# Slots without a loop, and mask products between two transpositions, in a fused "macaron" block

## What is computed

```python
def attn_layer(x, Wqkv, qs, ksc, Wo):            # x = shift_tokens(x)
    q, k, v = split(x @ Wqkv)                    # 16 heads of 64
    q, k = l2norm(q) * qs, l2norm(k) * ksc
    q, k = rotary with scale (q), rotary with 1/scale (k)
    # windows of 32: each query window sees its own and the previous key window
    sim = einsum('bhwie,bhwje->bhwij', q_win, k_two_wins) * 8.0
    sim = where(mask, -finfo.max, sim)           # i < j or i > j + 32
    out = softmax(sim) @ v_two_wins
    return out @ Wo
def ffn_layer(x, g, bln, W1, b1, W2, b2):
    a, gate = split((layernorm(x) * g + bln) @ W1 + b1)
    return a * gelu(gate) @ W2 + b2
for i in range(6):
    x = attn_layer(shift_tokens(x), ...) + x
    x = ffn_layer(shift_tokens(x), ...) + x
```

## Time and profile before

| | us |
|---|---|
| median of 3 runs | 3688.96 (3684.85 to 3690.24) |
| the profiled execution | 3686.52 |
| its span, first to last instruction | 3684.7 |
| PE busy | 3433.7 (93%) |
| DVE busy | 2845.5 (77%) |
| ACT busy | 2381.3 (65%) |
| POOL busy | 2333.4 (63%) |

### The profile page before, as it was taken

One profiled execution on the slowest core, in us unless ns is written; L12 is line 12 of the kernel. 1 busy time (PEld: TensorE's weight loads), 2 busy tenths in 40 slices (PEclk: granted clock), 3 DMA queues, 4 the chain that ended last, 5 costly groups with the idle time before them and its releaser, 6 DMA issues.

```text
span 3684.7 us, 129395 instructions
## 1 busy us (share of the span) xinstructions
PE 3433.7 (93%) x51660; PEld 1855.8 (50%) x51660; DVE 2845.5 (77%) x6042; ACT 2381.3 (65%) x4153; POOL 2333.4 (63%) x2187
## 2 busy tenths in 40 slices
PE   3799999999999999999797999999999999999997
PEld 2355554554554554555363555545545545545553
DVE  1788887887887887888367888878878878878883
ACT  1576776775776776677524667767767766766774
POOL 0677766766766776767145767667667766767661
PEclk6899999999999999999998999999999999999999
DMA  5000000000000000000100000000000000000000
GB/s 187 10 9 28 21 12 27 22 12 27 21 13 27 21 12 25 24 12 5 54 1 8 11 26 23 12 27 21 13 27 21 12 27 22 12 24 26 12 5 13
DMA packets 50151, 83.62 MB, mean 23 GB/s; under 512 B 7168, under 2 KB 37120, under 8 KB 47232
## 3 DMA queue, kind: packets, MB, share of 16 engines
q1 hardware_dynamic: 49536, 75.05, 6.5%
HBM read 67.69 MB, written 7.34 MB: 20 GB/s over the span
## 4 chain that ended last, share of the span: by engine, by line
PE 86%; issue 4%; DVE 4%; ACT 3%; POOL 1%; DMA 1%; SPq 0%; DVEq 0%; ACTq 0%; POOLq 0%
PE VS L890 19%; PE QA L830 18%; PE TB L849 10%; PE TB L914 7%; PE VS L937 7%; PE TB L873 6%; PE FB L963 3%; PE FB L964 3%; PE FB L972 3%; PE VS L928 2%; ACT KT L460 2%; PE TB L857 1%; PE FB L948 1%; PE FB L953 1%; DMA KT<-in_w_out 1%
## 5 line engine op out<-in xcount | busy, mean ns | idle before, releaser
L334 POOL TENSOR_TENSOR QN<-T 128x512 f32<-128x512 f32 x768 | 980.0, 1276 | 673.6 <-DVE T L606 673.6
L341 POOL TENSOR_TENSOR QN<-QN,RR 128x512 f32<-128x512 f32 x768 | 801.6, 1044 | 316.8 <-DVE RR L627 316.8
L830 PE MATMUL QA<-WQ,Y 128*128 128x512 f32 x1536 | 806.3, 622 | 68.7 <-DVE T L606 25.4
L890 PE MATMUL VS<-MW,Y 128*32 128x512 f32 x6144 | 738.8, 598 | 2.7 <-DVE Z L679 2.7
L446 ACT ACTIVATE SQ<-QA 128x512 f32<-128x512 f32 x768 | 458.6, 597 | 289.3 <-PE QA L830 254.5
L606 DVE TENSOR_TENSOR T<-QA,TAB 128x256 f32<-128x256 f32 x1536 | 571.0, 412 | 4.1 <-issue 4.1
L601 DVE TENSOR_TENSOR T<-QA,TAB 128x512 f32<-128x512 f32 x768 | 522.9, 681 | 48.2 <-issue 21.3
L466 ACT ACTIVATE V<-VS 128x512 f32<-128x512 f32 x768 | 461.1, 600 | 90.1 <-PE VS L890 89.5
L633 DVE TENSOR_TENSOR Y<-TB,Y 64x128 f32<-64x128 f32 x384 | 111.0, 289 | 521.0 <-PE TB L857 518.3
L614 DVE TENSOR_REDUCE SSQ<-SQ 128x8 f32<-128x512 f32 x768 | 486.8, 675 | 0.0
L914 PEld LDWEIGHTS TB<-CST,QN 128*128 128x128 f32 x3072 | 360.9, 142 | 220.9 <-issue 183.5
(11 more groups left out here) (172 smaller groups left out, 4260.2 us busy)
## 6 DMA issues: line engine op xcount, KB each, us to landing
TAB<-in_tables SPq DMA_DIRECT2D x192, 128.0 KB, 2.1
WQ<-in_w_qk SPq DMA_DIRECT2D x48, 256.0 KB, 3.2
MW<-m_dram SPq DMA_DIRECT2D x12, 1024.0 KB, 4.8
m_dram<-QN SPq DMA_DIRECT2D x6, 1024.0 KB, 4.9
W1R<-in_w SPq DMA_DIRECT2D x12, 341.0 KB, 3.4
KT<-in_w_vt SPq DMA_DIRECT2D x6, 512.0 KB, 5.8
KT<-in_w_out SPq DMA_DIRECT2D x6, 512.0 KB, 6.6
W<-in_w SPq DMA_DIRECT2D x12, 192.0 KB, 2.4
```

Of the source, the lines that this page charges most:

```text
L334: po.tensor_tensor(QN[:, n % 2, k, :], T1[:, k, :], T2[:, k, :], ALU.add).then_inc(s_add, 1)
L341: po.tensor_tensor(heads(QN[:, m % 2, k, :]), heads(QN[:, m % 2, k, :]), RR[:, m % 2, 8 * k:8 * k + 8].unsqueeze(2).to_broadcast([P, 8, DH ...
L830: mm(QA[:, k % 2, :], Y[:, j * P:(j + 1) * P], WQ[:, k, :], start=True, stop=True).then_inc(s_qk, 1)
L890: last = mm(VS[32 * q:32 * q + 32, w % 2, :], Y[:, a:a + WIN], MW[:, q, :], start=True, stop=True, tile_position=(0, 32 * q), skip_group_c ...
```

## The change

`all_slots` no longer has a loop: all 104 slots of a stack are written out, with constants in the waits. SyncE's conditions for the next layer's weights, which stood on the loop variable, are worked out from `c`, and `edge` is true for the same slots as before. Second, the two mask products leave `scores()` for a function of their own, `mask_scores()`, that is called right behind the transposition of the last keys and ahead of that of the last queries and of FFN-up. With them go the waits for VS (`s_ve`, and `s_z` in edge slots); the waits for the keys (`s_te3`, `s_kp`) stay in `scores()`.

```diff
         def all_slots(engine, slot, s):
-            for c in range(AHEAD):
-                slot(c, None, s)
-            with engine.Fori(0, DEPTH - 1) as it:
-                for c in range(AHEAD, AHEAD + TPL):
-                    slot(c, it, s)
-            for c in range(AHEAD + TILES - TPL, LAST):
+            for c in range(LAST):
                 slot(c, None, s)
...
-                if it is None:
+                if not AHEAD <= c < AHEAD + TILES - TPL:
                     return
-                nxt = bass.ds(it + 1, 1)
-                if c == AHEAD:
-                    sp.wait_ge(s_w1, by_layer(1, s * DEPTH, it, 1))
-                    sp.wait_ge(s_prb, by_layer(1, s * DEPTH, it, 1))
+                l = (c - AHEAD) // TPL + 1
+                nxt = slice(l, l + 1)
+                if c % TPL == AHEAD:
+                    sp.wait_ge(s_w1, by_layer(1, s * DEPTH + l - 1, it, 1))
+                    sp.wait_ge(s_prb, by_layer(1, s * DEPTH + l - 1, it, 1))
                     up_weights(nxt)
...
-                edge = it is None
+                edge = c < AHEAD or c >= AHEAD + TILES - TPL
...
+                def mask_scores():
+                    m = n - 2
+                    if edge:
+                        after(pe, s_z, 1, n - 3, 0, it, s)
+                    after(pe, s_ve, 4, n - 4, 3, it, s)
+                    for e in range(2):
+                        mm(VS[:, e, :].rearrange("p (a c k) -> p a c k", a=2, c=CH), IDB[:, :],
+                           MASKN[:, 0 if m % TPL == 0 else 1, :, :].unsqueeze(2).to_broadcast([P, 2, CH, WIN]),
+                           start=True, stop=False, skip_group_check=True)
+
                 def scores():
                     m = n - 2
                     j = m % 4
                     if j == 0 and m % TILES:
                         pe.wait_ge(s_kp, by_tile(1, m // 4, None) if it is None else it * 4 + m // 4)
-                    if edge:
-                        after(pe, s_z, 1, n - 3, 0, it, s)
-                    after(pe, s_ve, 4, n - 4, 3, it, s)
                     pe.wait_ge(s_te3, by_tile(1, m, it, 1))
-                    for e in range(2):
-                        mm(VS[:, e, :].rearrange("p (a c k) -> p a c k", a=2, c=CH), IDB[:, :],
-                           MASKN[:, 0 if m % TPL == 0 else 1, :, :].unsqueeze(2).to_broadcast([P, 2, CH, WIN]),
-                           start=True, stop=False, skip_group_check=True)
...
                 if live(c, 2, it):
                     qk_transpose(2, 3)
+                    mask_scores()
                 if live(c, 1, it):
                     qk_transpose(1, 2)
```

## The result

The changed kernel takes **3582.62 us** (median of four runs, 3580.02 to 3587.59), the kernel before 3689.6 us (median of its four runs beside it). The ratio is 0.9713 with a 95% interval of 0.9696 to 0.973. The forecast was 3581.0 us in a range of 3568 to 3615. The profiled execution took 3582.17 us, its span is 3580.4 us (3684.7 before).

What follows compares the result with a forecast made beforehand. PE, busy 93% of the span, was taken to bound the kernel. Terms: 70.1 + 42.8 - 3.8 - 6 + 4 = 107 us off the profiled 3686.52, giving 3579.5, as a median 3581 us; range 3568 to 3615.

Steps and rivals of the forecast that it cites:

- The branches: Slots behind the eight taken loop branches of PE: written out they become ordinary slots, 70.1 us gained.
- Rival 3: Branch slots: branches are cheap, the slot behind is long for a reason that stays; 3651 us, chance 0.03.
- The mask products: Masks moved between the two transpositions: 102 waits for the keys' copy go, 0.42 us each, 42.8 us gained.
- The thin margin of 0.11 us: Before the score products: PE arrives 1.40 us after the first transposition, keys' copy ends at 1.24, seen 0.05 later.
- rival 2: Mask's wait only changes place, keys' or V copy comes later; 42.8 us stay, costs paid; 3624 us, chance 0.07.
- The third cost: First FFN-up slot of each layer: attention products wait longer for the queries' copy, 12 x 0.5 = -6 us.
- Part three: Instruction fetch in written-out code: no new stalls before score products, half of the old ones gone, +4 us.
- rival 1: New written-out slots stall at the end slots' rate, 17 in 160 at 1.7 us, 28 us; 3613 us, chance 0.15.

Runs made afterwards that it cites:

- pe_looped: Kernel before with TensorE keeping its loop, the four other engines written out, mask products at their old place: 3654.64 us, ratio 0.9905.
- pe_written: Kernel before with only TensorE's slots written out, the other engines keeping their loop, mask products at their old place: 3678.86 us, ratio 0.9971.
- unroll_only: Changed kernel with the mask products back at their old place behind the wait for the last keys, slots written out: 3643.53 us, ratio 0.9876.
- split_waits: unroll_only with the two waits before the masks taken apart, only the second mask product waiting for the last keys: 3580.71 us, ratio 0.9693.

## Why the prediction was right, and where it was not

**The branches** were sized well: 70.1 us predicted, 72.0 measured over the eight slots, and its split between PE's standstill with a cold clock and DVE's own late code is what pe_looped (48.7 us) and pe_written (22.9 us) show. Rival 3, the cheap branch, is out: without the branches the slots are ordinary ones. The trace (3984 ns for a taken branch of PE, 76 ns for one that falls through) agrees with the Trainium skill's "Runtime: NRT & Kernel Launch" (Instruction fetch mechanics) that a branch out of the fetched window stalls.

**The mask products** gained what their term said: 0.42 or 0.43 us in each slot with centring or FFN-down, at a loss of 0.06 (predicted 0.04) in the others. The thin margin of 0.11 us before the score products held in all of them, so rival 2 is out. What the term missed is that their old place would have cost more in straight code than in the loop: unroll_only has 16 us more of extras, and 0.07 us more in 80 slots, that go away with the move. And split_waits shows that it need not have been a move: one wait per matmul at the old place does as well.

**The third cost** (12 x 0.5 = -6 us) failed as a step. "There I take 0.43 plus some 0.09" presumed that ScalarE's chain begins at the end of the FFN-up product with the table load, as the earlier trace rows show it for a loop slot. In straight code the load stands ahead of the wait. The trace of before had it: slot 9 to slot 10, already written out, takes 15.97 us where the loop's layers take 16.79. The order of ACT's instructions in the changed kernel shows it as well; the prediction went by PE's and DVE's. Ten slots gained 8.2 us: the step was off by 14 us.

**Part three** was right in the stacks' ends and failed in the new slots. "I take no new stalls and half of the old ones gone: +4 us": in the first and last slots the score products' waits for "issue" fell from 8.4 to 2.9 us; none of the five is left at its place, and two new ones came. In the slots that were a loop there are 12 new ones, 6.2 us, and 12 us more extras. The reason given against rival 1, that only the end slots have several waits before the dense products, overlooked that the loop's register waits become matmul waits when written out, so that pairs come together (`s_te3` with `s_kp` in every fourth slot; 7.4 of the 16.4 us lie there). Rival 1 was thus partly true: 12 new waits instead of 17, at 0.5 us each (6.2 / 12) instead of 1.7. Its rate was also taken too low: the 5 waits were divided by 48 end slots, but only 32 of them have score products (96 tiles in each stack, 80 of them in the loop), which makes 25 in 160 slots, 42 us.

So between slots 12 and 92 one step was 13 us too low (-5 for ten slots, +8.2 measured), the other 12 us too high, and they cancel: the terms of the prediction make 70.1 + 30 - 5 = 95 us there, measured are 99.5. Outside it was too high by 7 us (12 predicted, 4.9 measured). That the forecast fell within 2 us is luck of this kind; by its steps it was good to some 15 us. Nor do its parts hold one by one: written out alone, with the masks at their old place, the kernel gains 46 us where the terms say 74.

## What to carry to other kernels

When a loop is written out, read the waits on each matmul or activation in both versions, not only the order of the instructions: which wait sits on the instruction and which stands in the stream ahead of it can be worth nearly as much as the branches (63 us between unroll_only and split_waits, 72 us in the branch slots). In front of a dense run of small matmuls give each instruction one wait where you can, and put the second one on an earlier instruction. Look for the same place in the kernel where it is written both ways (here the stacks' first and last slots); the length of slot 9 to 10 there would have caught the third cost, and the five stalls in 32 slots were the better guide to straight code than the 160 loop slots.

## What was not expected of the hardware

- PE's fetch of the next 256 instructions is not always hidden. The 128 score products (256 instructions) take 1.48 us, and a boundary in or near them costs from nothing to 1.9 us; the waits before them are part of what decides. The Trainium skill's "Runtime: NRT & Kernel Launch" (Instruction fetch mechanics) calls the crossing of a 16 KiB boundary mostly hidden. In the 160 middle slots of split_waits the trace agrees (7.1 us of extras; the whole program has 411 packets of PE's code), in those of unroll_only it does not (32.7 us).
- Splitting the score products (64x32 tiles) in two with full-array transpositions between the halves costs 0.36 us a slot, for two changes more between small tiles and the full array.
- Parts that the kernels have in common (preparation, retention, a stack's last slots) differ by 1 to 5 us from kernel to kernel: retention with its borders took 208.4 to 214.2 us. Behind the last score products it was 64.2 to 69.5 us. Differences of that size between straight-code kernels say little on the edit.
